# An audio tower block rewritten: four batches at a time, transposed throughout, with a one-hot selection

## The reference

```python
# tok: keep the 204 rows of highest score, in order of score
scores = x @ w + b[0]
top_scores, top_indices = top_k(scores, 204)
h = take(x, top_indices) * sigmoid(top_scores)
# attn, one head, on layernorm(h); scale 1/8
q, k, v = s @ Wq.T + bq, s @ Wk.T + bk, s @ Wv.T + bv
mask = (q[:, :, 0] != 0) & (k[:, :, 0] != 0)
h = h + (softmax(q @ k.T * scale) masked by row @ v) @ Wo.T + bo
# ffn, on layernorm(h), normalised once more inside with gamma, beta
logits = xn @ Wr + br
w = softmax of the two largest logits, spread to 8 experts
h = h + sum over e of w[e] * (gelu(xn @ W1[e] + b1[e]) @ W2[e] + b2[e])
```

## Time and profile before

| | |
|---|---|
| median of 3 runs | 341.02 us (340.19 to 341.35) |
| the profiled execution | 340.78 us, of it 339.0 us span |
| mean granted clock of TensorE | 0.946 |
| TensorE busy | 279.1 us (82%) |
| VectorE busy | 250.0 us (74%) |
| ScalarE busy | 205.1 us (60%) |
| GpSimd busy | 186.3 us (55%) |
| moved by transfers | 8.79 MB |

### The profile page before, as it was taken

The page is one execution under the profiler, slowest core; times in us unless marked ns, Lnnn a source line. Parts: engine busy times, 40 slices in busy tenths (PEclk is TensorE's granted clock), DMA queues, the critical chain, the costliest instruction groups (busy, mean ns, idle before and its releaser), DMA issues. The chain is left out here.

```text
span 339.0 us, 6642 instructions
## 1 busy us (share of the span) xinstructions
PE 279.1 (82%) x1627; PEld 160.4 (47%) x1627; DVE 250.0 (74%) x912; ACT 205.1 (60%) x505; POOL 186.3 (55%) x195
## 2 busy tenths in 40 slices
PE   0423678878788789888889999999999999999992
PEld 0212567757566568567534353443435334343330
DVE  3758788998999997675736958778696877838323
ACT  1001356666758754898456776677777667767770
POOL 7368888888888888520104435355433535423342
PEclk9999978989979977999759999999999999999998
DMA  4124404200000001000000000000000000000001
GB/s 83 39 68 97 99 22 108 55 28 28 32 28 28 32 28 34 13 1 2 0 2 0 1 3 0 25 2 10 19 0 25 0 25 0 4 22 3 25 0 49
DMA packets 21099, 8.79 MB, mean 26 GB/s; under 512 B 12492, under 2 KB 20052, under 8 KB 21076
## 3 DMA queue, kind: packets, MB, share of 16 engines
q1 hardware_dynamic: 18452, 6.30, 7.8%
q0 software_dynamic: 2048, 2.10, 1.8%
q10 hardware_dynamic: 576, 0.13, 0.2%
HBM read 4.75 MB, written 3.77 MB: 25 GB/s over the span
## 5 line engine op out<-in xcount | busy, mean ns | idle before, releaser
L455 POOL TENSOR_TENSOR acc<-acc,ye 128x408 f32<-128x408 f32 x56 | 59.4, 1061 | 100.8 <-DVE ye L1124 100.4
L592 ACT ACTIVATE hid<-PS,b_eff 128x408 f32<-128x408 f32 x128 | 69.8, 597 | 17.1 <-PE PS L770 17.0
L430 POOL DMA_INDIRECT h_sorted<-h,row_of x64 | 65.5, 1023 | 21.8 <-issue 13.4
L770 PE MATMUL PS<-uT,w_g 64*128 64x408 f32 x256 | 62.7, 567 | 0.0
L797 PE MATMUL PS<-hid,w_sb 128*64 128x408 f32 x256 | 58.7, 537 | 0.0
L1124 DVE SCALAR_TENSOR_TENSOR ye<-PS,b_col,mb 128x408 f32<-128x408 f32 x56 | 35.7, 639 | 24.5 <-PE PS L797 24.3
L571 ACT ACTIVATE mb<-PS 128x408 f32<-128x408 f32 x64 | 32.6, 510 | 14.8 <-PE PS L761 11.8
L508 ACT ACTIVATE ET<-PS 102x408 f32<-102x408 f32 x32 | 16.4, 514 | 29.7 <-PE PS L664 22.3
L679 PE MATMUL PS<-k,qk 128*102 128x204 f32 x128 | 32.1, 406 | 0.0
L761 PE MATMUL PS<-mT,spread 128*128 128x408 f32 x64 | 29.1, 455 | 0.8 <-ACT mT L597 0.8
L551 ACT ACTIVATE E<-PS,nmax 102x204 f32<-102x204 f32 x64 | 26.7, 431 | 2.6 <-DVE nmax L973 2.6
(11 more groups left out here) (134 smaller groups left out, 539.4 us busy)
## 6 DMA issues: line engine op xcount, KB each, us to landing
H<-h_sorted SPq DMA_DIRECT2D x16, 102.0 KB
out<-y SPq DMA_DIRECT2D x8, 204.0 KB
h_sorted<-h,row_of POOLq DMA_INDIRECT x64
X<-in_x SPq DMA_DIRECT2D x2, 512.0 KB
X<-in_x SPq DMA_DIRECT2D x3, 256.0 KB, 3.9
w_raw<-in_L_ffn_W SPq DMA_DIRECT2D x2, 256.0 KB
X<-in_x SPq DMA_DIRECT2D x2, 128.0 KB, 4.2
w_sb<-in_L_ffn_W SPq DMA_DIRECT2D x1, 256.0 KB
```

What stands on the lines that cost most here:

```text
L430: pool.indirect_dma_start(out=h_sorted[:, :], out_offset=bass.IndirectOffsetOnAxis(ap=row_of[i][:, t:t + 1], axis=0), in_=h[i][:, t, :], i ...
L455: pool.tensor_tensor(acc[i][:, :], acc[i][:, :], ye[e % 2][:, :], ALU.add)\
L592: act.activation(hid[e % 2][c][:, :], hid_ps[e % 2][c][:, 0:C], ACT.Gelu, bias=b1_eff[:, e:e + 1]).then_inc(hid_ok, 1)
L770: pe.matmul(hid_ps[e % 2][c][:, 0:C], w1_g[rows, e, :], uT[i][rows, :], start=True, stop=True).then_inc(hidp_ok, 1)
```

## The change

The kernel is written anew. There are 8 units of four batches in both parts. x is loaded with two neighbouring rows of a batch in one partition (512 B pieces). GpSimd multiplies x with w (`weigh`), VectorE sums. The comparison is against `tie`, a matrix that holds minus a tiny number or zero by the order of indices, so that one operation over 256 columns gives the full rank of a row; the counting matmuls go. There is no way through memory for the rows: `one_hot` makes, for each of 8 tiles of 128 rows, a matrix with the gate's value where the rank equals the column, and TensorE multiplies x with it (`select`), which gives h transposed, two batches one above the other, in `H`. From there everything stays transposed: the mean is taken off by a matmul with `center` (identity minus block means), the variance comes from four narrow matmuls, VectorE adds eps, GpSimd raises to -0.5, and 8 small matmuls spread the result over the columns (`spread_std`, `spread_std2`, `spread_den` for one over the softmax's sum). Products in fp32r pairs become fp32 matmuls, with the two halves side by side where they fit.

The attention part has 13 steps with lags 0 to 5: 0 scores and one_hot, 1 select to spread_std, 2 normalise to softmax, 3 turn_exp to residual, 4 centre2 to spread_std2, 5 normalise2. In each step TensorE does turn_exp(0), select, score_rows(0), project, centre2, values, attend(0), centre, scores(0), turn_exp(1), variance2, score_rows(1), variance, attend(1), spread_den, scores(1), spread_std2, spread_std; VectorE does normalise, score_sum, normalise2, one_over_den, compare(0), gate_value, copy_v, row_max(0), var_eps2, compare(1), var_eps, one_hot, row_max(1), residual; GpSimd does weigh of the next unit, inverse_std2, inverse_std. The expert part starts when u of all units is there. The mixing weights no longer go through TensorE and ScalarE per expert: ScalarE copies the turned weights to `mT`, SP writes them to memory (`mixd`) and reads them back spread over 64 partitions for each half, for all 8 experts at once. Gelu is one instruction over both halves. Several small tensors of `route` lie in PSUM. Below, the core of the diff (comments and unchanged bodies left out).

```diff
-    PAIRS = B // 2
-    UNITS = PAIRS // 2
+    UB = 4
+    UNITS = B // UB
+    mixd = nc.dram_tensor("mixd", (UNITS, 2 * NE, C), fp32).ap()
...
+        A_LAG = 5
+        A_STEPS = UNITS + A_LAG
...
+            def send_mix(n):
+                sp.wait_ge(mT_ok, n + 1)
+                sp.dma_start(mixd[n], mT[:, :]).then_inc(mixd_ok, 16)
+                sp.wait_ge(mixd_ok, 16 * (n + 1))
+                if n >= 2:
+                    sp.wait_ge(ye_ok, NE * (n - 1))
+                for i, p in enumerate(halves):
+                    sp.dma_start(mb[n % 2][p, :, :].rearrange("p e c -> p (e c)"),
+                                 mixd[n, i * NE:(i + 1) * NE, :].rearrange("e c -> (e c)").partition_broadcast(D))\
+                        .then_inc(mb_in[n % 2], 16)
...
...
+                if (u := unit(s, 3)) is not None:
+                    copy_ET(u, 0)
+                if (u := unit(s, 1)) is not None:
+                    copy_hT(u)
+                if (u := unit(s, 2)) is not None:
+                    copy_qk(u)
...
+                if (u := unit(s, 2)) is not None:
+                    softmax(u, 0)
+                if (u := unit(s, 3)) is not None:
+                    copy_ET(u, 1)
+                    copy_rd(u)
+                if (u := unit(s, 2)) is not None:
+                    softmax(u, 1)
+                if (u := unit(s, 4)) is not None:
+                    copy_rb2(u)
+                if (u := unit(s, 1)) is not None:
+                    copy_rb(u)
...
+            def select(u):
+                pe.wait_ge(pick_ok, u + 1)
...
+                            last = pe.matmul(hT_ps[halves[p], cols(pr, 0, R)], X[:, u * UB + b, t * D:(t + 1) * D],
+                                             pick[:, b * T + t, :], start=(t == 0), stop=(t == T - 1))
...
+            def centre(u):
+                pe.wait_ge(hT_ok, u + 1)
...
+                pe.matmul(c_ps, center[:, :], H[:, u, :], start=True, stop=True).then_inc(cp_ok, 1)
...
+            def spread_std(u):
+                pe.wait_ge(rstd_ok, u + 1)
...
+                for g in range(G):
+                    for p in range(2):
+                        last = pe.matmul(rb_ps[halves[p], g * Q:(g + 1) * Q],
+                                         rstd[:, 2 * g + p:2 * g + p + 1].to_broadcast([Q, D]), ident[0:Q, 0:Q],
+                                         start=True, stop=True)
...
+            def turn_exp(u, pr):
+                pe.wait_ge(exp_ok, 2 * u + pr + 1)
+                if pr == 0:
+                    pe.wait_ge(rb_ok, min(u + 2, UNITS))
...
+            for k in range(K + 1):
+                n, e = divmod(k, NE)
+                if k < K:
+                    hidden(k)
+                if k >= 1:
+                    second(k - 1)
+                if k < K:
+                    if e == 1 and 2 <= n + 1 < UNITS:
+                        turn_mix(n + 1)
+                    if e == 3 and n >= 1:
+                        turn_back(n - 1)
+                    if e == 6 and n + 2 < UNITS:
+                        logits(n + 2)
...
+                    dve.scalar_tensor_tensor(out=ahead[:, i, :], in0=srow[:, b * N:(b + 1) * N], scalar=score[u % 2][:, g:g + 1],
+                                             in1=tie[:, t, :], op0=ALU.subtract, op1=ALU.is_gt,
+                                             accum_out=rank[u % 2][:, g:g + 1]).then_inc(cmp_ok, 1)
...
+                    last = dve.tensor_scalar(pick[:, g, :], row_no[:, :], rank[u % 2][:, g:g + 1], gate[u % 2][:, g:g + 1],
+                                             ALU.is_equal, ALU.mult)
...
+            for k in range(K):
+                n, e = divmod(k, NE)
+                weighted(k)
+                if e == 6 and n + 2 < UNITS:
+                    route(n + 2, 0)
+                if e == 7 and n + 2 < UNITS:
+                    route(n + 2, 1)
+                if e == 0 and 2 <= n + 1 < UNITS:
+                    route(n + 1, 2)
```

More of the change, by code:

```diff
@@ new lines, in scores @@
+            def scores(u, pr):
+                pe.wait_ge(q_ok, u + 1)
+                pe.wait_ge(k_ok, u + 1)
+                if pr == 0:
+                    pe.wait_ge(v_ok, u + 1)
+                else:
+                    pe.wait_ge(exp_ok, 2 * u + 1)
+                for qt in range(R):
+                    for p in range(2):
+                        last = pe.matmul(S_ps[:, p, qt * S:(qt + 1) * S], qT[halves[p], cols(pr, qt)],
+                                         kT[halves[p], cols(pr, 0, R)], start=True, stop=True)
+                last.then_inc(S_ok, 1)
@@ new lines, in logits @@
+            def logits(n):
+                pe.wait_ge(u_ok, n + 1)
+                pe.wait_ge(dve_prep, 5)
+                if n == 0:
+                    pe.wait_ge(cmp_ok, TU * UNITS)
+                else:
+                    pe.wait_ge(mT_ok, n)
+                if n >= 3:
+                    pe.wait_ge(y_ok, n - 2)
+                for g in range(G):
+                    last = pe.matmul(lg_ps[:, 2 * NE * g:2 * NE * (g + 1)], uT[:, n, g * Q:(g + 1) * Q],
+                                     wr_bd[:, :, :].rearrange("p a e -> p (a e)"), start=True, stop=True)
+                last.then_inc(lgp_ok, 1)
@@ new lines, in turn_mix @@
+            def turn_mix(n):
+                pe.wait_ge(top, TOP * (n + 1))
+                for g in range(G):
+                    last = pe.transpose(mT_ps[:, g * Q:(g + 1) * Q],
+                                        mix[:, 2 * g:2 * g + 2, :].rearrange("q a e -> q (a e)"), ident[0:Q, 0:Q])
+                last.then_inc(mTp_ok, 1)
+            pe.wait_ge(pool_prep, 4)
+            score_rows(0, 0)
+            prepare_attn()
+            score_rows(0, 1)
+            pe.wait_ge(dve_prep, 4)
@@ new lines, in hidden, with second @@
+            def hidden(k):
+                n, e = divmod(k, NE)
+                if k >= 2:
+                    pe.wait_ge(hid_ok, k - 1)
+                for p in range(2):
+                    last = pe.matmul(hid_ps[k % 2][:, p, 0:C], w1_g[halves[p], e, :], uT[halves[p], n, :],
+                                     start=True, stop=True)
+                last.then_inc(hidp_ok, 1)
+            def second(k):
+                e = k % NE
+                pe.wait_ge(hid_ok, k + 1)
+                if k >= 2:
+                    pe.wait_ge(ye_ok, k - 1)
+                for p in range(2):
+                    last = pe.matmul(y_ps[k % 2][halves[p], :], w2_sb[:, e, :], hid[k % 2][:, p, :], start=True, stop=True)
+                last.then_inc(yp_ok, 1)
```

1619 lines of the change are left out of this document (700 added, 919 removed).

## The result

The changed kernel took 379.0 us (median of 4 runs, 377.9 to 380.57) against 341.19 for the kernel before: ratio 1.111, 95% interval 1.105 to 1.117. The forecast was 373, its own range 358 to 392. The profiled execution has a span of 376.8 us.

The account below looks back on a forecast made before the run. Before, VectorE with GpSimd behind it paced attention, TensorE the experts. Changed: attention chain 201 + first weights 2.5 + experts 139 + tail 8.5 = 351 us span, 353 with 1.8 around it; clock adds 11 and 9: 373 us, range 358 to 392.

Parts of the forecast that it names:

- The attention step is a chain: Attention part: dependent operations across engines, closed by the wait on rb_ok, set a full step at 19.2 us.
- TensorE's load: Attention part: TensorE's work per step of four batches sums to 16.0 us, below the chain's 19.2.
- the one-hots: Attention part, VectorE: eight one-hots of 204 columns cost 2.2 us of a 13.6 us load per step.
- The clock in the attention part: Attention part: new TensorE gaps lower the granted clock, 1.5 us per step over 7.5 full steps, 11 us.
- The 1.73 us per expert: Expert part: TensorE's remaining matmuls, 0.89 + 0.84 us per expert, set the pace; 64 experts give 110.7 us.
- The stall in front of `turn_mix`: Expert part: TensorE waits about 2.9 us per unit for VectorE's route, queued behind weighted(0); paid for six units.
- The clock term of 1.5 per unit: Expert part: gaps lower the granted clock, adding 1.5 us per stalled unit, 9 us in all.
- The 2.5 us for the first unit's weights: Start of the expert part: unit 0's spread weights have no cover, so 2.5 us is added once.
- The spread weights: Expert part: store about 4 us, loads 6.9 plus 2 to land; ready at 19 us, wanted at 19.7, just in time.
- Rival (c): Expert part: spread weights come late at half the rate, seven units by 6 to 7 us; 416 us, chance 0.13.
- Rival (b): Whole kernel: the clock holds because steps are denser than before; 353 us, still slower, chance 0.20.
- Rival (d): Attention and expert parts: steps run at TensorE's 16.0 us and full clock; 338 us, full step below 16.4, chance 0.15.

Follow-up runs that it names:

- the clock held: Changed kernel plus dummy TensorE matmuls, 14 before each of steps 2 to 9 and 5 before attend(1): 374.53 us, ratio 1.093.
- the three orders: Changed kernel with ScalarE's rb copies before softmax(u, 1), row_max(u, 1) before one_hot, and turn_mix one expert later: 354.64 us, ratio 1.040.
- 77 dummies: Against the three orders with the early start and 124 dummy matmuls in TensorE's start and end attention waits, cut to 77: 339.37 us, ratio 0.997.
- the early start: Changed kernel with unit 1's logits, routing and turn moved into unit 0's experts, copy_mT(0) to the start of step 11: 377.84 us, ratio 1.108.

## Why the prediction was right, and where it missed

**The attention step is a chain: right in mechanism, a little small in size.** The chain was named with its links. With the clock held, steps 3 to 8 took 117.0 us against 113.5 forecast (18.0, 76.8 and 18.7), the full steps 19.4 to 20.3 against 19.2. The wait on `rb_ok` opens the step, and moving it gave the largest single gain. TensorE's load was below my 16.0: it is busy for 15.3 of 18.3 us in the step of the three orders that has the full clock; the spreads cost 0.75 to 0.87, not 1.1.

**VectorE's queue: a link left out.** I priced the one-hots at 2.2 us of load and put them nowhere in the chain. They stand in front of row_max(1), and beside GpSimd's product they took 4.4 us; that is the 1.6 us (5.6 against 4.0) by which the step's last piece is longer with the clock held. Keeping the product away gave 8.5 us. Moving the one-hots behind the maximum gave 7, but takes them away from the product too, so the two gains can't be added.

**The clock in the attention part: mechanism right, size too small.** The term was 1.5 us per step; it measured about 2.2, and in the steps around (start to step 3, steps 10 to 12) I had entered nothing. There lie 3.9 and 4.4 of the 17.5 us that the attention part was longer than forecast. Between 174 and 217 us of the kernel with the three orders the granted clock is 0.50, and holding the clock up there and at the start gave 6.5 us even with too much fill. The rows of 168 to 172 us, the same place in the kernel before, had shown a clock of 0.50; I used them for the full steps only.

**The expert part: the stall right, its size and its clock too large.** The 1.73 us per expert measured 1.72. The stall in front of `turn_mix` was forecast at 2.9 and is 2.13: weighted(0) ended 1.3 us after its matmul (248.78 + 0.63 against 248.13) instead of 1.85, and the four small operations took 0.85, not 1.0. Six units, 4.6 us. Small VectorE operations at 0.25 were right, also beside GpSimd. The clock term of 1.5 per unit came in two units of six: 3.2 us, not 9. Taking the stall away gave 10.6 us in all. The 2.5 us for the first unit's weights did not fall on TensorE: VectorE waited 5.5, but with two output buffers TensorE went on without a gap. These three make 13 us, less about 1.5 for the slow first expert.

**The spread weights: right.** Loads of 8.9 us forecast, 8.2 measured; the store about 1.5 rather than 4 (253.06 to 254.56). Rival (c) did not come true, but was real in kind: at twice the bytes it costs 55 us.

**Rival (b), the clock holds, 353:** the clock did not hold (0.854 over the span, against 0.946 before). With the dummies in the steps, steps 3 to 9 came near their sum (133.4 against 129.4), but the attention part as a whole did not: the first hidden matmul stood at 223.7 us against 201. **Rival (d), 338:** no full step fell below 17.5 us in any of the kernels, against the 16.4 that it needed; the chain decides.

**What stays open.** Which waits bring the low clock and which don't is not settled. In the changed kernel the first matmuls of a step had the duration of 1.2 GHz after waits of 4.04, 3.71, 2.53 and 2.54 us, and that of 2.4 GHz after 1.15, 1.18 and 2.21; but 2.13 us in front of `turn_mix` were followed by the low clock in two of six units, and about 1 us in front of attend(1) in some steps and not in others. What bounds the full-clock step of 18.3 us in the kernel with the three orders was read from the trace (the residual behind the one-hots), not tried. How GpSimd's product lengthens the one-hots is open too.

## What to carry to other kernels

Write out, for every engine whose result the chain waits for, what stands ahead of it in that engine's queue; a load that is "only 2 us" lengthens the step as soon as the chain stands behind it, and it may be longer beside another engine than alone. When long steps replace many short overlapping ones, price the low clock in every bare stretch, those at the start and the end of the pipeline first. Work that holds the clock up must fit into the wait: 77 dummies gained more than 124. And when a gain in one place depends on the clock, try it again after the gaps are closed: the early start was worth 1 us before and some 2 to 4 after.

## What the runs showed of the hardware

- An fp32 VectorE operation with one SBUF matrix and two scalars per partition (128 x 204, 378 ns) takes up to 1415 ns where a GpSimd product of 128 x 512 in SBUF falls among such operations; with that product kept away, 386 at most. GpSimd's inverse root of 102 x 8 (1.79 us) beside eight of them cost nothing: 2.46 us.
- A broadcast load of 816 KB to 64 partitions, two at once, lands in 8.2 us; four at once, the last two in 14.8.
- A step of 23.33 us in which TensorE was busy for 19.75 had a mean granted clock of 0.79. The same wait of 2.13 us in the expert part was followed by matmuls at 1.2 GHz in two of six units and at 2.4 GHz in four; one of about 1 us in front of attend(1) was followed by either (100.94 and 119.26 with the three orders).
